# Scatters of the linear layer issued a pair at a time, and the routing steps packed three to a chunk

## The reference

```python
x = x + _layernorm(_L0_attn_ref(_layernorm(x), ...))
x = x + _layernorm(_L0_ffn_ref(_layernorm(x), ...))
x = x + _layernorm(_L1_attn_ref(_layernorm(x), ...))   # linear attention, 16 heads of 64, causal
x = x + _layernorm(_L1_ffn_ref(_layernorm(x), ...))    # top 2 of 8 experts, each with a capacity
```

## Time and profile before

| | us |
|---|---|
| median of 3 runs (lowest, highest) | 4883.49 (4867.18, 4885.91) |
| the profiled execution's own time | 4889.14 |
| its span, first to last instruction | 4887.3 |
| TensorE busy | 4197.2 (86% of the span) |
| VectorE busy | 2655.3 (54%) |
| ScalarE busy | 1880.3 (38%) |
| GpSimd busy | 997.1 (20%) |

### The profile page before, as it was taken

One profiled execution on the slowest core, in us unless ns is written; L12 is line 12 of the kernel. 1 busy time (PEld: TensorE's weight loads), 2 busy tenths in 40 slices (PEclk: granted clock), 3 DMA queues, 4 the chain that ended last, 5 costly groups with the idle time before them and its releaser, 6 DMA issues. The chain is left out here.

```text
span 4887.3 us, 75209 instructions
## 1 busy us (share of the span) xinstructions
PE 4197.2 (86%) x26100; PEld 3101.1 (63%) x26100; DVE 2655.3 (54%) x7794; ACT 1880.3 (38%) x2968; POOL 997.1 (20%) x1028
## 2 busy tenths in 40 slices
PE   5999999999975999999999999999998599999920
PEld 2344444444434777777777777777777598899920
DVE  4787787787734444544434455443444454454546
ACT  1565566566553322333333233333322233233300
POOL 3233334242322111111111111111111000000056
PEclk8998998898877999999999999999999799999965
DMA  4353334334302000000000000000000222121147
GB/s 71 67 89 72 58 67 81 53 68 84 63 18 70 9 12 15 19 18 16 10 15 10 10 14 14 13 10 13 12 4 8 67 65 81 63 62 58 48 125 160
DMA packets 174527, 221.54 MB, mean 45 GB/s; under 512 B 26860, under 2 KB 151755, under 8 KB 174144
## 3 DMA queue, kind: packets, MB, share of 16 engines
q1 hardware_dynamic: 135360, 163.41, 15.1%
q0 software_dynamic: 12288, 26.83, 2.2%
q10 hardware_dynamic: 26496, 26.22, 1.6%
HBM read 94.03 MB, written 77.73 MB: 35 GB/s over the span
## 5 line engine op out<-in xcount | busy, mean ns | idle before, releaser
L758 ACT ACTIVATE probs<-a_scores 128x1024 f32<-128x1024 f32 (+3 forms) x768 | 615.1, 811 | 395.2 <-PE a_scores L662 388.9
L919 DVE CUSTOM_DVE_ANT_0 a_scores<-a_scores,mask 128x384 f32<-128x384 f32 (+3 forms) x1024 | 481.3, 515 | 131.3 <-PE a_scores L648 124.1
L1831 DVE TENSOR_TENSOR l_a<-l_general,l_a 128x512 f32<-128x512 f32 x64 | 44.3, 692 | 743.3 <-PE l_general L1338 743.3
L662 PEld LDWEIGHTS a_scores<-q_st,k_st 50*128 50x128 f32 x1536 | 154.4, 198 | 420.6 <-issue 298.0
L231 POOL TENSOR_TENSOR l_ln_rstd<-l_ln_ve,minus_half 128x4 f32<-128x4 f32 x80 | 83.3, 1041 | 1520.2 <-DVE l_ln_ve L204 1520.2
L662 PE MATMUL a_scores<-q_st,k_st 50*128 50x512 f32 (+3 forms) x1536 | 362.1, 469 | 34.9 <-issue 26.1
L922 DVE TENSOR_REDUCE mx<-a_scores 128x2 f32<-128x1024 f32 x256 | 311.9, 1224 | 129.6 <-PE a_scores L648 128.6
L682 PE MATMUL a_out<-probs,v_aug 128*32 128x512 f32 (+3 forms) x3072 | 359.1, 543 | 2.0 <-POOL probs L851 1.9
L648 PE MATMUL a_scores<-k_st,q_st 48*128 48x512 f32 (+3 forms) x1536 | 315.4, 409 | 47.0 <-ACT probs L758 28.7
L2134 PE MATMUL e_out<-e_weights_hi,e_hT_lo 128*128 128x256 f32 x1088 | 304.1, 279 | 0.0
L2134 PE MATMUL e_out<-e_weights_lo,e_hT_hi 128*128 128x256 f32 x1088 | 304.0, 279 | 0.0
(11 more groups left out here) (232 smaller groups left out, 9769.1 us busy)
## 6 DMA issues: line engine op xcount, KB each, us to landing
q_st<-parts SPq DMA_DIRECT2D x192, 128.0 KB, 4.6
k_st<-parts SPq DMA_DIRECT2D x192, 128.0 KB, 6.6
expert_rows_scratch<-zero SPq DMA_DIRECT2D x8, 2176.0 KB, 12.9
e_weights<-in_L_ffn_W_dram SPq DMA_DIRECT2D x16, 1024.0 KB, 6.4
e_rows<-expert_rows_scratch SPq DMA_DIRECT2D x24, 384.0 KB, 3.3
expert_out_scratch<-e_y ACTq DMA_DIRECT2D x24, 384.0 KB, 2.6
x_in<-in_L_attn_x_dram SPq DMA_DIRECT2D x8, 1024.0 KB, 5.4
x_res<-in_L_attn_x_dram SPq DMA_DIRECT2D x8, 1024.0 KB, 5.5
```

The source lines that it names most:

```text
L662: last = nc.tensor.matmul(psum_r[:, R.slot(u), h2, 0:w], k_st[rows, 2 * hg + pair, i * P:(i + 1) * P], q_st[rows, 2 * hg + pair, q0:q0 + w ...
L758: nc.scalar.activation(probs[:, k % 3, 2 * pair:2 * pair + 2, 0:w], psum_r[:, R.slot(u), :, 0:w], ACT.Exp).then_inc(R.evacuated[R.slot(u)], 1)
L919: last = nc.vector.tensor_tensor_reduce(s, s, mask[:, HALF - w:HALF], 1.0, LEAST, ALU.add, ALU.max, out[:, h2, :])
```

## The change

- `scatter` takes a range of tiles and a flag `spaced`. When it is set, each tile's pair of DMAs after the first waits until the pairs before have landed on both semaphores.
- GpSimd's order becomes: power 0 of `ln1`, the wait for `to`, the pair of tile 0, power 1 of `ln1`, the pairs of tiles 1 to 3 (each after the landing of the ones before), a wait for the last landing, `low`. In the very last scatter all eight DMAs still go out in a row.
- `rows` now shares its bytes with `nT1["lo"]`, which GpSimd itself writes, so VectorE's wait for the landings goes, and GpSimd does it ahead of `low`.
- The routing steps are three to a chunk: `choose` in chunks 0 to 3, the count at chunk 6, `locate` in chunks 7 and 8. The places in a chunk are: 0, between the denominators' maximum and the wait for it; 1, after the division; 2, after the state's addition.
- The semaphore `scatter_next` is only counted up; nothing waits on it.

```diff
@@ -1145,9 +1145,10 @@
         norm = sb("l_norm", [P, G4, D])
 
 
+        nT1 = {"hi": sb("l_nT1_hi", [P, CD, HALF], F32R)}
         with nc.sbuf_tensor("l_rows", [P, G4, D], F32) as rows:
             pass
-        nT1 = {part: sb(f"l_nT1_{part}", [P, CD, HALF], F32R) for part in ("hi", "lo")}
+        nT1["lo"] = sb("l_nT1_lo", [P, CD, HALF], F32R)
         nT2 = sb("l_nT2", [P, CD, HALF])
         qT = sb("l_qT", [P, NP, HALF])
         kT = sb("l_kT", [P, NP, HALF])
@@ -1231,11 +1232,12 @@
         to_ready = sem("l_to_ready")
         scatter_begun = sem("l_scatter_begun")
         rows_gone = sem("l_rows_gone")
+        scatter_next = sem("l_scatter_next")
         x2_read = sem("l_x2_read")
         scattered = [sem(f"l_scattered{k}") for k in range(2)]
         route_chain = Chain(sem, "l_route_chain", 18)
 
-        COUNT_AT = 8
+        COUNT_AT = 6
         x3_stored = sem("l_x3_stored")
         a3_ready = sem("l_a3_ready")
         a3_normed = sem("l_a3_normed")
@@ -1636,12 +1638,18 @@
                             "p (j d) -> p j d", j=1).broadcast_to([P, G4, D]), ALU.mult
                         ).then_inc(rows_ready, 1)
 
-                def scatter(g, src, copied=True):
-                    if copied:
-                        pool.wait_ge(rows_ready, g + 1)
-                    pool.wait_ge(to_ready, g + 1)
-                    pool.sem_inc(scatter_begun, 1)
-                    for j in range(G4):
+                def scatter(g, src, tiles, spaced):
+                    if 0 in tiles:
+                        if spaced:
+                            pool.wait_ge(rows_ready, g + 1)
+                        pool.wait_ge(to_ready, g + 1)
+                        pool.sem_inc(scatter_begun, 1)
+                    for j in tiles:
+                        if spaced and j:
+
+                            for k in range(2):
+                                pool.wait_ge(scattered[k], (g * G4 + j) * 16)
+                            pool.sem_inc(scatter_next, 1)
                         for k in range(2):
                             nc.gpsimd.indirect_dma_start(
                                 out=rows_dram,
@@ -1654,10 +1662,17 @@
                         last_norms(g - 1, 1 - s)
                         keep_rows(g - 1, g, U)
                     if not last_group:
-                        for call in range(2):
-                            ln1.power(pool, g + 1, call)
+                        ln1.power(pool, g + 1, 0)
                     if not first:
-                        scatter(g - 1, rows)
+                        scatter(g - 1, rows, range(1), True)
+                    if not last_group:
+                        ln1.power(pool, g + 1, 1)
+                    if not first:
+                        scatter(g - 1, rows, range(1, G4), True)
+
+                        for k in range(2):
+                            pool.wait_ge(scattered[k], g * G4 * 16)
+                        pool.sem_inc(rows_gone, 1)
                     if not last_group:
                         low(g + 1)
                     ln2.power(pool, g, 0)
@@ -1678,7 +1693,7 @@
                 low_weights(2)
                 groups(pool, group)
                 last_norms(NGR - 1, 1)
-                scatter(NGR - 1, norm, copied=False)
+                scatter(NGR - 1, norm, range(G4), False)
                 for k in range(2):
                     pool.wait_ge(scattered[k], NGR * G4 * 16)
 
@@ -1836,8 +1851,16 @@
                     for i in range(2):
                         G.wait_evacuated(dve, g, u0 + i)
 
-                CHOOSE = {n: (2 * n, 2 * n + 1) for n in range(6)}
-                LOCATE = {COUNT_AT + 1 + n: (2 * n, 2 * n + 1) for n in range(3)}
+
+                CHOOSE = {n: 3 * n for n in range(4)}
+                LOCATE = {COUNT_AT + 1 + n: 3 * n for n in range(2)}
+                assert COUNT_AT > 3
+
+                def route(g, n, place):
+                    if n in CHOOSE:
+                        choose(g, CHOOSE[n] + place)
+                    elif n in LOCATE:
+                        locate(g, LOCATE[n] + place)
 
                 def group(g, b, s, U, first, last_group):
 
@@ -1865,11 +1888,9 @@
                         den_chain.at = 2 * n
                         den_chain.mark(nc.vector.tensor_scalar(den[:, 0, :], num[:, :, DH1],
                                                                EPS_DEN, None, ALU.max))
-                        if not first and n in LOCATE:
-                            locate(g - 1, LOCATE[n][0])
+                        if not first:
+                            route(g - 1, n, 0)
                         den_chain.wait(dve, g)
-                        if not first and n in CHOOSE:
-                            choose(g - 1, CHOOSE[n][0])
                         den_chain.link(dve, g, nc.vector.reciprocal(den[:, 1, :], den[:, 0, :]))
                         nc.vector.tensor_tensor(
                             o[:, j % 2, g4 * 4 * DH1:(g4 + 1) * 4 * DH1].rearrange(
@@ -1878,10 +1899,8 @@
                             den[:, 1, :].rearrange("p (h a) -> p h a", a=1).broadcast_to([P, 4, DH1]),
                             ALU.mult).then_inc(NUM.evacuated[NUM.slot(n)], 1)
 
-                        if not first and n in CHOOSE:
-                            choose(g - 1, CHOOSE[n][1])
-                        if not first and n in LOCATE:
-                            locate(g - 1, LOCATE[n][1])
+                        if not first:
+                            route(g - 1, n, 1)
                         NUM.wait_evacuated(dve, g, n)
                         UP.wait_full(dve, g, n)
                         if n == COUNT_AT and not first:
@@ -1892,12 +1911,9 @@
                             st = state[rows, 2 * g4:2 * g4 + 2, cols]
                             last = nc.vector.tensor_tensor(st, st, up[rows, :, cols], ALU.add)
                         last.then_inc(UP.evacuated[0], 1)
+                        if not first:
+                            route(g - 1, n, 2)
                     if not last_group:
-                        if not first:
-
-                            for k in range(2):
-                                dve.wait_ge(scattered[k], g * G4 * 16)
-                            dve.sem_inc(rows_gone, 1)
                         high(g, g + 1, U)
                     add_a3(g, s, U["W"])
                     chain2.at = 0
```

## The result

| | us |
|---|---|
| changed kernel, median of 4 runs (lowest, highest) | 4759.48 (4753.28, 4763.35) |
| kernel before beside it, median of 4 runs (lowest, highest) | 4884.51 (4867.18, 4885.91) |
| ratio of the two, 95% interval | 0.9751 (0.9726 to 0.9775) |
| profiled execution after: own time, span | 4763.35, 4761.6 |

The change makes the kernel 125 us faster. The forecast was 4790 us in a range of 4770 to 4854: right in sign and in the cause of the waits, too cautious by 31 us, and 10.5 us outside the range.

A forecast was written before the change was run, and what follows sets the result against it. The prediction took the linear layer's TensorE-VectorE loop to be held up by signals late during back-to-back scatters. It summed 4889.1 - 103 + 7 + 2 = 4795 us, 4790 as a median, range 4770 to 4854.

The forecast's parts named there:

- The cause of the waits: Linear layer: TensorE's signals reach other engines late while scatters follow without a break; VectorE's "remote" waits sum to 84.4 us.
- The threshold of three: From group 15: three scatters back to back start the lateness, two don't; 0.92 us late after the third.
- Pairs, -103 us: Linear layer, groups 1 to 15: lateness ends, each group falls back to group 0's stretch of 24.69 us; 103 us saved.
- What stays in the pairs, +7 us: Lateness left inside pairs: 0.1 to 3.7 us a group, taken at 0.5, so 7 us in 15 groups.
- GpSimd's waits cost nothing: GpSimd's queue: power 1 some 3 us later with 5 us of cover, `low` with over 10 us; cost nothing.
- Routing, +2 us: Routing steps three to a chunk on VectorE: +0.15 us a group, 2 us in all, range -10 to +18.
- The sum: Whole kernel: profiled 4889.1 us with the terms gives 4795; as a median, 5.6 us less, 4790.
- lower end: Low end of the range, 4770 us: no lateness left and routing at its best.
- inner upper bound: The forecast's own upper bound, 4790 + 18 + 7 = 4815 us, before the range was widened to 4854.

The follow-up runs named there:

- before_again: The kernel before, unchanged, run again in a comparison without late signals: 4768.2 us, ratio 0.9994.
- spacing_only_c: The kernel before with the spaced pairs alone and the old routing, where signals came late: 4761.05 us in one run, the kernel before 4887.9.
- spacing_only: The kernel before with the spaced pairs alone and the old routing, first run, without late signals: 4767.1 us, ratio 0.9994.
- rolling: The kernel before, old routing, each scatter waiting only for the landing of the one two before it, without late signals: ratio 0.9999.
- rolling_b: The kernel before, old routing, each scatter waiting only for the one two before it to land, where signals came late: 4774.25 us, ratio 0.9784.
- half_rows: The kernel before with each scatter writing only the first half of each row, without late signals: ratio 1.0007.
- routing_only: The kernel before with the three-to-a-chunk routing alone, eight scatters still in a row, without late signals: 4762.6 us, ratio 0.9983.
- routing_only_b: The kernel before with the three-to-a-chunk routing alone, another run without late signals: ratio 0.9991.
- after_again: The changed kernel, unchanged, run again in a comparison without late signals: 4756.8 us, ratio to the kernel before 0.9971.
- rolling_three: The changed kernel, each scatter waiting only for the one two before it to land in place of pairs, without late signals: 4767.2 us, ratio to before 0.9994.
- after_third: The changed kernel once more, where signals came late: 4768.6 us, ratio to the kernel before 0.9767.
- spacing_only_b: The kernel before with the spaced pairs alone and the old routing, another run without late signals: ratio 0.9965.
- routing_only_c: The kernel before with the three-to-a-chunk routing alone, where signals came late: 4903.4 us, ratio 1.0037.
- fours: The changed kernel with one wait for landings in place of three, so two runs of four scatters, where signals came late: 4807.7 us, ratio to before 0.9845.
- half_rows_b: The kernel before with each scatter writing only half of each row, where signals came late: 4884.5 us in one run, the kernel before 4887.9.

## Why the forecast had the sign and missed the size

**The cause of the waits: right.** TensorE's signals were late because of scatters back to back. `before_again` adds a condition that the first trace could not show: only in some comparisons. Between the two kinds the kernel before differs by 2276.6 - 2174.7 = 102 us in the linear layer and some 115 us in the median.

**The threshold of three: not a sharp one.** The prediction read from one place in group 15 that two scatters in a row make nothing late. With the pairs and the old routing (`spacing_only_c`) no signal is over 0.1 us late. With the new routing and pairs some are up to 0.84 us late, and with the rolling rule one is 1.9. Four in a row reach 2.4 us, eight 5.8.

**The terms by groups.** From the first mask of a group to that of the next is a group's period, read from the timelines; its median over the 15 periods of an execution leaves single disturbed groups out. Where signals are at most 0.5 us late it is 134.76 to 134.81 us in seven executions with the old routing (`before_again`, the three of `spacing_only`, `rolling`, `rolling_b`, `half_rows`), and 134.30 to 134.32 in four with the new one (`routing_only`, `routing_only_b`, `after_again`, `rolling_three`). The kernel before has about 141.1 and 142.0 to 142.4 in turn where they are late (140.2 once), the kernel after 134.74, and 134.79 in `after_third`.

**Pairs, -103 us: right.** Groups 1 to 14 of the kernel before stand 95.2 us above 134.8 each in sum. From group 15's first mask to the experts pass 158.8 us, and 153.4 in `before_again`, 5.4 more (I had 6.4 for this group): 100.6. And `spacing_only_c` is back at 134.8, with a stretch of 10.63 us where I took group 0's 10.64.

**What stays in the pairs, +7 us: right in size, by luck.** With both halves of the change a lateness of 0.1 to 0.8 us is left, mostly at two masks of a group, and the period stands 134.74 to 134.79 against 134.3: 0.45 us a group for my 0.5. But 0.5 was a choice between 0.1 and 3.7, and with the pairs alone nothing of it is there (134.81 us).

**GpSimd's waits cost nothing: right.** `low` waits for VectorE in group 2. In group 1 it waits for the landings, and the product still starts 10.64 us after the last mask.

**Routing, +2 us: wrong in sign, within its bounds.** Where no signal is late it takes off 0.5 us a group, 7 in 14. I had priced only where the steps lie on VectorE, and put the new place 2 at a loss. Which of the chunks gains is not settled by the runs.

So the linear layer's terms should have read -100.6 + 7 - 7 = -100.6, for -102.3 measured. The small rest is in single groups that take 1.4 to 1.7 us more than their neighbours, zero to three of them in an execution and not in the same places; they put 5.5 us between `spacing_only` (2180.2) and `spacing_only_b` (2174.7).

**The sum: the step that failed.** It read 4889.1 - 103 + 7 + 2 = 4795, and the profiled execution took 4763.35. The terms of the linear layer came to -94 for a measured -102.3, mostly by the sign of the routing term. The other 23.5 us of the miss come from the first number. I took the profiled execution's softmax layer for a constant because no edit touches it, and gave a change in it neither a term nor a place in the range. It isn't one: over 18 profiled executions of kernels with the same softmax layer it took 1530 to 1575 us. (The part behind the linear layer is no constant either, 1040 to 1048 us over the 18; the first two profiles agreed in it to 0.1 us.) Two stretches of 31 us tell how. TensorE's clock there, before:

```profile
587.00:618.00 31.00, 26.26 (x130) 11.93 (x132) 17.52 (x42) 12.82 (x17) 3.90 (x6) 0.51 0.49 105
757.00:788.00 31.00, 25.61 (x128) 11.64 (x128) 17.97 (x46) 12.82 (x18) 4.61 (x7) 0.50 0.52 108
```

and after:

```profile
587.00:618.00 31.00, 30.47 (x195) 14.81 (x192) 26.96 (x77) 18.31 (x23) 6.30 (x9) 0.88 0.28 77
757.00:788.00 31.00, 30.84 (x208) 14.92 (x204) 28.35 (x89) 17.94 (x25) 6.05 (x8) 0.98 0.23 56
```

From about 415 to 1135 us the clock falls to 1.2 GHz every 163 to 175 us. Mostly it stays there for 14 us or for 31 (in some executions 27), and one execution can have both: the five stretches are all of 31 us before, as in the whole of both rows above, and three of 14 and two of 31 after. Three stretches shorter by 17 us, at half the clock, are worth some 25 us, an estimate from these rows. Two terms therefore explain the profiled execution: 4889.1 - 102.3 - 23.5 = 4763.3, and it measured 4763.35. The range failed at the same place. Its lower end took only the bounds of the edits, while the three runs of the kernel before already lay 18.7 us apart. Its inner upper bound, 4790 + 18 + 7 = 4815, counts the routing's 2 us twice and should be 4813; nothing rests on it.

**What stays open.** Why TensorE's signals are late in some comparisons and not in others; no trace shows the path. And whether the softmax layer is shorter by chance. Before, `routing_only_c`, `fours` and `half_rows_b`, whose signals were late, have 1563 to 1575 us; the five executions in such comparisons that had pairs or the rolling rule have 1536 to 1553; but the nine in other comparisons range over both, 1530 to 1568. Of the kernels beside late signals that gained, each gained more in the median than in the linear layer (the first: 125 and 102), so part of it may belong to the change, though it comes earlier in the execution. No run was made that tells this apart.

## What to carry to other kernels

Where an engine waits for a release that the profile calls "remote", put its wait beside the issues of GpSimd's indirect DMAs. If three or more are under way, issue them in pairs, each after the landing of the pair before: that costs nothing where GpSimd has the time, was worth 97 us here in comparisons of one kind, and did no harm in the other. Measure the kernel before on several occasions and chips ahead of any forecast, and give a layer that no edit touches its own spread in the range.

## What the hardware showed that was not expected

- The same kernel takes 4769 to 4773 us in some comparisons and 4878 to 4890 us in others; whether the chip decides it is not shown. With eight scatters in a row TensorE's signals arrive at most 0.1 us late in the first kind and up to 5.8 us late in the second, while VectorE's, in the place shown, reach TensorE within 0.05 us. Half the bytes change nothing (2276.8 us of linear layer against 2276.6).
- A layer whose instructions and data are the same took from 1530 to 1575 us from one execution to another, in the main by how long its stretches at 1.2 GHz last, most of them 14 us or 31.
